# Conv-attention hybrid: the FFN's down product and fp8 cast re-placed, two mix chunks moved among the second turns

## The chip, the cores and the metric

The kernel runs on one core of one Trainium2 chip, in one launch. The metric is device time in microseconds, the median of several runs. Engines are called by name: TensorE (PE), VectorE (DVE), ScalarE (ACT), GpSimd (POOL) and SyncE (SP), which issues all DMAs of the part that is looked at here. They run side by side and are ordered only by semaphores; each executes its own list in order.

## The reference

Input x has shape (64, 55, 55, 96), float32. Cut to what matters:

```
x = conv(x) * x + bias + x               # depthwise, 9x9 taps at distance 3, centre left out
t = tokens(x)                            # (64, 3025, 96)
h = relu(bn1(ln(t) @ w1.T))              # 192 channels
X = fft(h, axis=tokens)                  # complex, 3025 points
y = real(ifft(relu(Xr*rd - Xi*id + rb) + 1j*relu(Xi*rd + Xr*id + ib)))
t = t + bn2(y @ w2.T)
u = f16(q8(ln(t)) @ q8(W1).T) + q8(b1)   # 384 channels, rounded to f16
t = t + f16(q8(relu(u)) @ q8(W2).T) + q8(b2)
```

q8 rounds to the 8-bit float with 5 exponent bits. The layer norms have no gain and no bias.

## The kernel before

Stage one is the convolution, with bands of weights as matrices. Stage two, `mixer_stage`, handles one image per part and keeps four images in flight. Part i does: the token rows of image i (`first`: transposes `turn`, product `widen`, 121-point transform `rows`), the 25-point transform `columns`, the gates and the `mix` with w2 and the `inverse` of image i-1 (`second`), the second inverse transform `inverse_rows` and the residual of image i-2 (`prep`), and the FFN of image i-3 (`third`). Parts 4 to 62 are one loop, `Fori`; parts 0 to 3 and 63 to 66 are written out with the missing pieces left away. Parts 3 to 64 have both `second` and `third`.

An image has 3025 tokens as 25 steps of 121. The FFN goes over them in seven chunks, CHUNK = 0, 4, 8, 12, 16, 19, 22, 25: four chunks of four steps and three of three. The 31 pairs of frequencies for `mix` and `inverse` are cut in seven as well: MIXED = 0, 5, 10, 15, 19, 23, 27, 31, so three chunks of five pairs and four of four. One mix pair is the products of L1034 and L1036.

On every engine a part is two halves. The first is a loop over 14 half chunks for image i, with the eight gate tiles of image i-1 put between them at TILE_AT. In it GpSimd adds and clips for the gates (L664, L667), VectorE combines them (L864, L865, L868, L875). The second half is what the change touches:

- Second turns (TensorE, L1054): seven transposes of the normalised tokens of image i-3, into banks 4 and 5; ScalarE copies each to `xq` (L748), and the turn of chunk c waits for the copy of chunk c-2. mix(0) stands ahead of turn 4. mix(0) waits for `v_ready`, `s_ready` and `d_ready` of all eight gate tiles.
- FFN loop, TensorE, slot c from 0 to 9: mix(c) unless it is 0, up(c) (L1078, three products into banks 4, 5, 6), inverse(c-1) (L1065), inverse_rows(c-3) (L958), down(c-1) (L1094, all into bank 7).
- ScalarE, slot c from 0 to 7: out_w2(c) (L757, mixed from the mix), wide(c) (L771, the up product to `y16`), out_inverse(c-1) (L763), narrow(c-1) (L779, the down product to `z16`).
- VectorE, slot c from 0 to 9: residual(c-3) (L885) and the layer-norm statistics of the chunk before it (L800), then for c below 7 the bias and relu of `y16` in place (L924, three instructions) and the cast to `hq` (L930); in slots 0 and 3 also statistics of the next image's tokens.
- GpSimd, chunk by chunk: bias b2 to `z16` (L675), sum with `t2` into `o_sb` (L678). SP stores `o_sb` to the output.

Buffers set these waits: up(c) waits for wide(c-1); wide(c) waits for the cast of chunk c-2 (`hq_ready`), since `y16` has two buffers; down(c) waits for the cast of chunk c and for narrow(c-1) (`z_ready`); the cast of chunk c waits for down(c-2) (`f2_done`); mix(c) waits for out_w2(c-2) and inverse(c) for out_w2(c); residual(c) waits for inverse_rows(c) and for `o_sb` of chunk c of image i-3 (`o_ready`), because both use `t2`. In the next part, columns(0) waits for five residuals and columns(1) for all seven.

Of the kernel before, what the change touches and what calls it, by code (L numbers as in the profile page):

```python
# [98 lines left out]
U = 121  # L99
# [7 lines left out]
NC = 7  # L107
CHUNK = (0, 4, 8, 12, 16, 19, 22, 25)
MIXED = (0, 5, 10, 15, 19, 23, 27, 31)
# [3 lines left out]
TILES = 8  # L113
KC = 8
# [4 lines left out]
LAG = 3  # L119
EARLY = 3  # L120
ROOT_C = 3
TILE_AT = (0, 2, 4, 6, 7, 9, 10, 12)


# [166 lines left out]
def mixer_stage(nc, x1, p, a_d, g_d, out):  # L291
    with ExitStack() as ctx:
# [3 lines left out]
        def sem(name):  # L296
            return ctx.enter_context(nc.semaphore(name))
# [35 lines left out]
        y16 = [sb(f"y16{s}", [128, FM, TOK], F16) for s in range(2)]  # L333
        hq = [sb(f"hq{s}", [128, FM, TOK], F8) for s in range(2)]
# [172 lines left out]

        act_passed = sem("act_passed")
        pe_passed = sem("pe_passed")
        dve_passed = sem("dve_passed")  # L510
        pool_passed = sem("pool_passed")
        sp_passed = sem("sp_passed")
        t_loaded = sem("t_loaded")
# [14 lines left out]
        s_ready = sem("s_ready")  # L528
        d_ready = sem("d_ready")
# [14 lines left out]
        relu_ready = sem("relu_ready")  # L544
        hq_ready = sem("hq_ready")
        f2_done = sem("f2_done")
# [7 lines left out]
        def ring(b, c, n=NC):  # L554

            return b * n + max(c - 1, 0)
# [96 lines left out]
        @block.gpsimd  # L653
        def _(pool):
            b2 = b2q[:, :].unsqueeze(1).broadcast_to([U, JC, C])

            def part(i, first, second, prep, third, more):
                if second:
                    b = i - 1
                    for t in range(TILES):  # L660
                        p0, p1, _, hf = group(t)
                        pool.wait_ge(m_ready, b * TILES + t + 1)
                        sv = spec[0:HH, hf, p0:p1, 0:Q // 2]
                        nc.gpsimd.tensor_tensor(sv, sv, gate_buffer(gc, t), ALU.add).then_inc(s_ready, 1)  # L664
                        pool.wait_ge(v_ready, b * TILES + t + 1)
                        pool.sem_inc(pool_passed, 1)
                        nc.gpsimd.tensor_scalar(gate_buffer(gv, t), gate_buffer(gv, t), 0.0, None,  # L667
                                                ALU.max).then_inc(v_cut, 1)
                if third:
                    b = i - 3  # L670
                    for c in range(NC):
                        pool.wait_ge(z_ready, b * NC + c + 1)
                        c0, c1 = CHUNK[c], CHUNK[c + 1]
                        z = z16[c % 2][:, 0:c1 - c0, :]
                        nc.gpsimd.tensor_tensor(z, z, b2[:, 0:c1 - c0, :], ALU.add).then_inc(z_biased, 1)  # L675
                        pool.wait_ge(z_biased, b * NC + c + 1)
                        pool.wait_ge(o_stored[c % 2], slot_uses(b, c) * 16)
                        nc.gpsimd.tensor_tensor(o_sb[c % 2][:, 0:c1 - c0, :], t2[:, c0:c1, :], z,  # L678
                                                ALU.add).then_inc(o_ready, 1)

            run_all(pool, part)
# [4 lines left out]
        def _(act):  # L686
# [6 lines left out]
            def part(i, first, second, prep, third, more):  # L693
# [46 lines left out]
                if third:  # L740
                    b = i - 3
# [32 lines left out]
                def narrow(c):  # L774
                    b = i - 3
                    act.wait_ge(f2_done, b * NC + c + 1)
                    act.wait_ge(o_ready, ring(b, c))
                    n = CHUNK[c + 1] - CHUNK[c]
                    nc.scalar.activation(z16[c % 2][:, 0:n, :].rearrange("p j c -> p (j c)"),  # L779
                                         ps[0:U, 7, 0:n * C], ACT.Copy).then_inc(z_ready, 1)  # L780

                for c in range(NC + 1):
                    if second and c < NC:
                        out_w2(c)
                    if third and c < NC:
                        wide(c)
                    if second and c:
                        out_inverse(c - 1)
                    if third and c:
                        narrow(c - 1)  # L790
                    if more and c == ROOT_C - 1:
                        root(0, i + 1)

            run_all(act, part)

        @block.vector
        def _(dve):
# [42 lines left out]
            def part(i, first, second, prep, third, more):  # L840
# [73 lines left out]
                for c in range(NC + LAG):  # L914
                    if prep and c >= LAG:
                        residual(c - LAG)
                        if c > LAG:
                            residual_stats(c - LAG - 1)
                    if third and c < NC:
                        b = i - 3  # L920
                        dve.wait_ge(y16_ready, b * NC + c + 1)
                        n = (CHUNK[c + 1] - CHUNK[c]) * U
                        for m in range(FM):
                            last = nc.vector.tensor_scalar(y16[c % 2][:, m, 0:n], y16[c % 2][:, m, 0:n],  # L924
                                                           b1q[:, m:m + 1], 0.0, ALU.add, ALU.max)
                        last.then_inc(relu_ready, 1)
                        dve.wait_ge(f2_done, ring(b, c))
                        dve.wait_ge(relu_ready, b * NC + c + 1)
                        dve.sem_inc(dve_passed, 1)
                        nc.vector.tensor_copy(hq[c % 2][:, :, 0:n], y16[c % 2][:, :, 0:n],  # L930
                                              saturate=False).then_inc(hq_ready, 1)
                    if more and c < 4 - EARLY:
                        n = EARLY + c
                        dve.wait_ge(t_loaded, (i + 2) * 16)
                        last = stats(tok, 0, PART[n], PART[n + 1])
                        if n == 3:
                            variance(0, i + 1, last)
                    if more and c == ROOT_C:
                        inverse_root(0, i + 1)
                        deviation(i + 1)  # L940
# [6 lines left out]
        def _(pe):  # L947
            def part(i, first, second, prep, third, more):
# [73 lines left out]
                            turn(h // 2 + 1)  # L1022
                def mix(c):
                    b = i - 1
                    if c == 0:
                        pe.wait_ge(v_ready, b * TILES + TILES)
                        pe.wait_ge(s_ready, b * TILES + TILES)
                        pe.wait_ge(d_ready, b * TILES + TILES)
                    if c >= 2:
                        pe.wait_ge(w2_ready, b * NC + c - 1)  # L1030
                    for p in range(MIXED[c], MIXED[c + 1]):
                        n = p - MIXED[c]
                        o = ps[0:Q, c % 2, n * C:(n + 1) * C]
                        nc.tensor.matmul(o, spec[0:HH + 1, 0, p, :], w2t[0:HH + 1, 0, :],  # L1034
                                         start=True, stop=False)
                        last = nc.tensor.matmul(o, spec[0:HH, 1, p, :], w2t[0:HH, 1, :],  # L1036
                                                start=False, stop=True)
                    last.then_inc(w2_done, 1)

                if third:  # L1040
                    b = i - 3
                    if first:
                        pe.wait_ge(turned_used, (i + 1) * NC)
                        pe.wait_ge(hid_ready, (i + 1) * HALVES)
                    else:
                        pe.wait_ge(y16_ready, b * NC)
                    for c in range(NC):
                        if second and c == 4:
                            mix(0)
                        pe.wait_ge(xn2_ready, b * NC + c + 1)  # L1050
                        if c >= 2:
                            pe.wait_ge(xq_ready, b * NC + c - 1)
                        for j in range(CHUNK[c + 1] - CHUNK[c]):
                            last = nc.tensor.transpose(ps[0:C, 4 + c % 2, 128 * j:128 * j + U],  # L1054
                                                       xn2[:, CHUNK[c] + j, :], ident[0:U, 0:U])
                        last.then_inc(turned2, 1)
# [40 lines left out]
                    last.then_inc(f2_done, 1)  # L1097

                for c in range(NC + LAG):
                    if second and c < NC and not (third and c == 0):  # L1100
                        mix(c)
                    if third and c < NC:
                        up(c)
                    if second and 1 <= c <= NC:
                        inverse(c - 1)
                    if prep and c >= LAG:
                        inverse_rows(c - LAG)
                    if third and 1 <= c <= NC:
                        down(c - 1)

            run_all(pe, part)

# [39 lines left out]
```

## Time and profile before

| | us |
|---|---|
| median of 3 runs | 6206.72 (6203.02 to 6210.03) |
| profiled execution | 6218.28 |
| its span, first to last instruction | 6216.1 |
| granted TensorE clock, mean over the span | 0.951 |
| TensorE busy with products | 5297.6 |
| VectorE busy | 4527.8 |
| ScalarE busy | 3248.1 |
| GpSimd busy | 1951.5 |

The convolution fills the time up to about 1044 us. From there on one part follows another, one image every 77.5 to 78.6 us. An engine's busy time is a sum over stages with different limits, so the rows further down are of one image, the one whose second turns begin at 3003.59 us. Times in a timeline are starts; several instructions of one group are merged into one row; pipelined products overlap, so the distance of two starts can be shorter than the duration.

### The profile page before, as it was taken

Reading aid. Unit: us, or ns where it says so; the run is one execution under the profiler, and the core shown is the slowest. Engines: PE = TensorE matmul, PEld = TensorE weight load, DVE = VectorE, ACT = ScalarE, POOL = GpSimd, SP = SyncE. Lnnn points to the kernel's source line nnn. Section 1 sums busy time; section 2 is a strip of 40 time slices with the busy share of each in tenths; the row PEclk is TensorE's granted clock in tenths of the full one; section 3 lists DMA queues with packets and bytes.
Section 4 is the critical chain, followed back from the end, with each engine's and each line's share of the span. In section 5 each row is a group of like instructions: output and inputs, shape, how many; then the busy total and the mean of one; then the engine's idle time right before and its main releaser. Section 6 shows DMA issues by size and latency. Waiting matters only on the chain. (4 is left out here: it accounts for less than half of the span.)

```text
span 6216.1 us, 136648 instructions
## 1 busy us (share of the span) xinstructions
PE 5297.6 (85%) x44298; PEld 4566.4 (73%) x44298; DVE 4527.8 (73%) x12660; ACT 3248.1 (52%) x6469; POOL 1951.5 (31%) x1924
## 2 busy tenths in 40 slices
PE   8999996488888888888888888888888888888887
PEld 8889996377777777777777777777777777777775
DVE  4555664457777777777777777777777777777776
ACT  0000000256666666666666666666666666666664
POOL 0000000123333333434333343334333333333343
PEclk9999998689999999999999999999999999999995
DMA  6665655355555555555555555555555555555552
GB/s 223 180 188 171 193 171 161 85 137 140 139 137 137 141 137 136 141 142 139 139 139 138 140 139 141 142 141 139 140 140 141 139 140 142 139 136 138 139 139 55
DMA packets 681435, 892.28 MB, mean 144 GB/s; under 512 B 240785, under 2 KB 629130, under 8 KB 659530
## 3 DMA queue, kind: packets, MB, share of 16 engines
q1 hardware_dynamic: 610124, 800.99, 50.7%
q10 hardware_dynamic: 71174, 89.35, 4.7%
q8 instruction: 100, 1.64, 0.1%
q14 instruction: 37, 0.30, 0.0%
HBM read 505.60 MB, written 384.61 MB: 143 GB/s over the span
## 5 line engine op out<-in xcount | busy, mean ns | idle before, releaser
L664 POOL TENSOR_TENSOR spec<-spec,gc 96x400 f32<-96x400 f32 (+1 forms) x512 | 488.7, 955 | 2473.3 <-DVE spec L864 2473.3
L1007 PEld LDWEIGHTS ps<-fb,acol 100*96 100x96 f32 x7936 | 778.8, 170 | 316.0 <-DVE gv L868 233.7
L1007 PE MATMUL ps<-fb,acol 100*96 100x100 f32 x7936 | 815.4, 257 | 124.2 <-DVE gv L868 116.2
L675 POOL TENSOR_TENSOR z<-z,b2q 121x384 f16<-121x384 f16 (+1 forms) x448 | 397.4, 887 | 1560.0 <-ACT z L779 1560.0
L989 PE MATMUL ps<-hid,fa 121*128 121x384 f32 (+1 forms) x1792 | 708.6, 477 | 187.5 <-DVE arow L854 106.7
L707 ACT ACTIVATE hid<-ps,rstd 121x192 f32<-121x192 f32 x1600 | 602.7, 432 | 482.8 <-PE ps L978 482.6
L1034 PE MATMUL ps<-w2t,spec 97*100 97x96 f32 x3968 | 718.2, 264 | 19.1 <-DVE spec L875 19.1
L259 DVE SCALAR_TENSOR_TENSOR xout<-cps,xin 114x351 f32<-114x351 f32 (+3 forms) x512 | 402.4, 786 | 443.0 <-PE cps L286 443.0
L1036 PE MATMUL ps<-w2t,spec 96*100 96x96 f32 x3968 | 702.3, 260 | 0.0
L667 POOL TENSOR_SCALAR gv<-gv 96x400 f32<-96x400 f32 (+1 forms) x512 | 663.9, 1297 | 106.4 <-DVE gv L868 106.3
L854 DVE COPY arow<-ps 128x384 f32<-128x384 f32 (+1 forms) x896 | 454.3, 507 | 323.9 <-PE ps L989 293.7
L282 PE MATMUL cps<-xin,toep 114*114 114x117 f32 (+3 forms) x3072 | 615.6, 283 | 85.2 <-DMA xin<-in_x 71.9
L978 PE MATMUL ps<-w1t,xnt 97*121 97x192 f32 x3200 | 680.7, 330 | 0.7 <-ACT xnt L698 0.7
L1094 PEld LDWEIGHTS ps<-w2q,hq 128*121 128x121 fp8e5 x4800 | 326.5, 139 | 420.3 <-issue 394.7
L924 DVE TENSOR_SCALAR y<-y,b1q 128x484 f16<-128x484 f16 (+1 forms) x1344 | 521.7, 444 | 120.2 <-ACT y L771 112.7
L771 ACT ACTIVATE y<-ps 128x1452 f16<-128x1452 f32 (+1 forms) x448 | 561.0, 1252 | 56.2 <-PE ps L1078 43.1
L1094 PE MATMUL ps<-w2q,hq 128*121 128x96 fp8e5 x4800 | 350.0, 222 | 269.3 <-issue 263.7
L1034 PEld LDWEIGHTS ps<-w2t,spec 97*100 97x100 f32 x3968 | 544.3, 176 | 39.6 <-issue 29.3
L286 PE MATMUL cps<-xin,toep 114*114 114x96 f32 (+1 forms) x3072 | 570.4, 268 | 0.0
L488 ACT ACT_TABLE_LOAD x1 | 1.3, 1283 | 1078.8 <-PEq L164 1078.8
L978 PEld LDWEIGHTS ps<-w1t,xnt 97*121 97x121 f32 x3200 | 514.7, 185 | 55.4 <-ACT xnt L698 1.0
L1036 PEld LDWEIGHTS ps<-w2t,spec 96*100 96x100 f32 x3968 | 537.2, 176 | 0.0
(101 smaller groups left out, 11296.9 us busy)
## 6 DMA issues: line engine op xcount, KB each, us to landing
a_d<-arow SPq DMA_DIRECT2D x256, 384.0 KB, 3.6
acol<-a_d SPq DMA_DIRECT2D x64, 1200.0 KB
grow<-g_d SPq DMA_DIRECT2D x128, 600.0 KB, 7.4
tok<-x_d SPq DMA_DIRECT2D x64, 1134.4 KB
t_res<-x_d SPq DMA_DIRECT2D x64, 1134.4 KB
acol<-a_d SPq DMA_DIRECT2D x64, 1125.0 KB
a_d<-arow SPq DMA_DIRECT2D x192, 288.0 KB, 5.1
xin<-in_x SPq DMA_DIRECT2D x256, 211.5 KB, 5.7
```

Of the source, the lines that this page charges most:

```text
L282: nc.tensor.matmul(o[0:GP, :], toep[0:GP, ch, GP:2 * GP], xs[:, pad:pad + cols], start=True, stop=False)
L286: last = nc.tensor.matmul(o[0:GP, 0:cols - step + pad], toep[0:GP, ch, 0:GP], xs[:, step + pad:], start=False, stop=True)
L667: nc.gpsimd.tensor_scalar(gate_buffer(gv, t), gate_buffer(gv, t), 0.0, None, ALU.max).then_inc(v_cut, 1)
L707: last = nc.scalar.activation(hid[h % 2][:, j, :], ps[0:U, 5 + h % 2, j * H:(j + 1) * H], ACT.Relu, scale=rstd[0][:, s0 + j:s0 + j + 1])
L771: nc.scalar.activation(y16[c % 2][:, :, 0:n], ps[:, 4:4 + FM, 0:n], ACT.Copy).then_inc(y16_ready, 1)
L924: last = nc.vector.tensor_scalar(y16[c % 2][:, m, 0:n], y16[c % 2][:, m, 0:n], b1q[:, m:m + 1], 0.0, ALU.add, ALU.max)
L978: last = nc.tensor.matmul(ps[0:U, 5 + h % 2, j * H:(j + 1) * H], xnt[c % 2][:, 2 * (h % 2) + j, :], w1t[:, :], start=True, stop=True)
L989: nc.tensor.matmul(ps[0:M, 7, 0:n * H], fa[:, :], hid[h % 2][:, 0:n, :].rearrange("p j h -> p (j h)"), start=True, stop=True).then_inc(a_d ...
L1007: last = nc.tensor.matmul(ps[0:HH, 2 - 2 * (t % 2) + n // 4, 128 * (n % 4):128 * (n % 4) + Q], acol[:, p0 + n, hf * HH:(hf + 1) * HH], fb[ ...
L1034: nc.tensor.matmul(o, spec[0:HH + 1, 0, p, :], w2t[0:HH + 1, 0, :], start=True, stop=False)
L1036: last = nc.tensor.matmul(o, spec[0:HH, 1, p, :], w2t[0:HH, 1, :], start=False, stop=True)
L1094: last = nc.tensor.matmul(ps[0:U, 7, C * j:C * (j + 1)], hq[c % 2][:, m, j * U:(j + 1) * U], w2q[:, m, :], start=(m == 0), stop=(m == FM - 1))
```

## The change

Three edits, all in the FFN half of a part.

- TensorE: the call of down moves from the end of slot c, as down(c-1), to the head of slot c, as down(c-2). ScalarE: narrow(c-1) becomes narrow(c-2), and its loop gets a ninth slot.
- mix(0) stands ahead of second turn 2 and mix(1) ahead of second turn 4. The mix of chunk c waits for the `s_ready` and `d_ready` of only those gate tiles that cover its pairs, each chunk for its own.
- The cast from `y16` to `hq` goes from VectorE to GpSimd. GpSimd's list becomes: cast 0, cast 1, then for each chunk c: cast c+2, bias c, sum c. The cast keeps its waits. The semaphore that counted VectorE's passes goes away.

```diff
@@ gpsimd
+                def cast(c):
+                    b = i - 3
+                    n = (CHUNK[c + 1] - CHUNK[c]) * U
+                    pool.wait_ge(f2_done, ring(b, c))
+                    pool.wait_ge(relu_ready, b * NC + c + 1)
+                    pool.sem_inc(pool_passed, 1)
+                    nc.gpsimd.tensor_copy(hq[c % 2][:, :, 0:n], y16[c % 2][:, :, 0:n],
+                                          saturate=False).then_inc(hq_ready, 1)
+
                 if third:
                     b = i - 3
+                    cast(0)
+                    cast(1)
                     for c in range(NC):
+                        if c + 2 < NC:
+                            cast(c + 2)
                         pool.wait_ge(z_ready, b * NC + c + 1)
@@ scalar
-                for c in range(NC + 1):
+                for c in range(NC + 2):
                     if second and c < NC:
                         out_w2(c)
                     if third and c < NC:
                         wide(c)
-                    if second and c:
+                    if second and 1 <= c <= NC:
                         out_inverse(c - 1)
-                    if third and c:
-                        narrow(c - 1)
+                    if third and c >= 2:
+                        narrow(c - 2)
@@ vector
-                        dve.wait_ge(f2_done, ring(b, c))
-                        dve.wait_ge(relu_ready, b * NC + c + 1)
-                        dve.sem_inc(dve_passed, 1)
-                        nc.vector.tensor_copy(hq[c % 2][:, :, 0:n], y16[c % 2][:, :, 0:n],
-                                              saturate=False).then_inc(hq_ready, 1)
@@ tensor
                 def mix(c):
                     b = i - 1
+                    tiles = 2 * ((MIXED[c + 1] - 1) // KC) + 2
                     if c == 0:
                         pe.wait_ge(v_ready, b * TILES + TILES)
-                        pe.wait_ge(s_ready, b * TILES + TILES)
-                        pe.wait_ge(d_ready, b * TILES + TILES)
+                    pe.wait_ge(s_ready, b * TILES + tiles)
+                    pe.wait_ge(d_ready, b * TILES + tiles)
@@ tensor, second turns
-                        if second and c == 4:
-                            mix(0)
+                        if second and c in (2, 4):
+                            mix(c // 2 - 1)
@@ tensor, FFN loop
                 for c in range(NC + LAG):
-                    if second and c < NC and not (third and c == 0):
+                    if third and 2 <= c < NC + 2:
+                        down(c - 2)
+                    if second and c < NC and not (third and c < EARLY_MIX):
                         mix(c)
                     if third and c < NC:
                         up(c)
...
                         inverse_rows(c - LAG)
-                    if third and 1 <= c <= NC:
-                        down(c - 1)
```

EARLY_MIX is 2.

## Rows read from the trace of the kernel before

**Rows 1.** The page: busy time, share of the span and instructions of each engine.
```profile
PE 5297.6 (85%) x44298; PEld 4566.4 (73%) x44298; DVE 4527.8 (73%) x12660; ACT 3248.1 (52%) x6469; POOL 1951.5 (31%) x1924
```

**Rows 2.** Waits: who waited for whom, total us, times, longest.
```profile
PE ps L1094 <- issue: 263.7, 251, 2.5
```

**Rows 3.** Timeline, TensorE, one image's FFN: start, duration, instructions, [idle before].
```profile
3003.59 0.99 PE L1054 MATMUL ps<-ident,xn 121*96 121x121 f32 x8
3005.00 1.60 PE L1054 MATMUL ps<-ident,xn 121*96 121x121 f32 x8 [0.42 <-ACT xq L748]
...
3009.26 0.78 PE L1054 MATMUL ps<-ident,xn 121*96 121x121 f32 x6
...
3011.70 0.77 PE L1078 MATMUL ps<-xq,w1q 96*128 96x484 fp8e5 x3 [0.74 <-ACT xq L748]
...
3014.07 0.78 PE L1078 MATMUL ps<-xq,w1q 96*128 96x484 fp8e5 x3
...
3015.94 0.84 PE L1094 MATMUL ps<-w2q,hq 128*121 128x96 fp8e5 x12 [0.21 <-issue]
3016.62 0.38 PE L1034 MATMUL ps<-w2t,spec 97*100 97x96 f32 x2
...
3018.42 0.78 PE L1078 MATMUL ps<-xq,w1q 96*128 96x484 fp8e5 x3
...
3023.36 0.78 PE L1078 MATMUL ps<-xq,w1q 96*128 96x484 fp8e5 x3
...
3027.64 0.63 PE L1078 MATMUL ps<-xq,w1q 96*128 96x363 fp8e5 x3
...
3031.59 0.63 PE L1078 MATMUL ps<-xq,w1q 96*128 96x363 fp8e5 x3
...
3036.15 0.63 PE L1078 MATMUL ps<-xq,w1q 96*128 96x363 fp8e5 x3
...
3042.09 0.68 PE L1094 MATMUL ps<-w2q,hq 128*121 128x96 fp8e5 x9 [2.19 <-issue]
...
3044.46 1.01 PE L969 MATMUL ps<-ident,tok 121*97 121x121 f32 x4
```

**Rows 4.** Timeline, ScalarE, the same image, same columns.
```profile
3011.08 0.47 ACT L748 ACTIVATE xq<-ps 96x363 fp8e5<-96x363 f32 x1 [0.39 <-PE ps L1054]
...
3012.50 1.38 ACT L771 ACTIVATE y<-ps 128x1452 f16<-128x1452 f32 x1 [0.50 <-PE ps L1078]
...
3020.51 0.56 ACT L763 ACTIVATE mixed<-ps 100x480 f32<-100x480 f32 x1
3022.11 0.49 ACT L779 ACTIVATE z<-ps 121x384 f16<-121x384 f32 x1 [1.04 <-PE ps L1094]
```

**Rows 5.** Groups of instructions of VectorE and GpSimd: busy us, mean ns | idle before.
```profile
L885 DVE TENSOR_TENSOR t<-ps,t_res 121x384 f32<-121x384 f32 (+1 forms) x448 | 228.5, 510 | 322.7 <-PE ps L958 287.7 <-POOL o_sb L678 34.8
...
L667 POOL TENSOR_SCALAR gv<-gv 96x400 f32<-96x400 f32 x384 | 510.4, 1329 | 82.3 <-DVE gv L868 82.3
```

**Rows 6.** Timeline, VectorE and GpSimd, the same image.
```profile
3003.73 0.57 DVE L868 SCALAR_TENSOR_TENSOR gv<-ps,nrd,gq 96x350 f32<-96x350 f32 x1
...
3013.92 0.86 DVE L924 TENSOR_SCALAR y<-y,b1q 128x484 f16<-128x484 f16 x3 [1.34 <-ACT y L771]
3020.21 0.92 DVE L930 CAST hq<-y 128x1452 fp8e5<-128x1452 f16 x1
3030.90 0.91 POOL L675 TENSOR_TENSOR z<-z,b2q 121x384 f16<-121x384 f16 x1 [1.37 <-ACT z L779]
3034.46 0.73 DVE L800 BATCH_NORM_STATS2 bn<-t 121x6 f32<-121x96 f32 x4
3039.17 0.73 POOL L675 TENSOR_TENSOR z<-z,b2q 121x288 f16<-121x288 f16 x1 [1.39 <-ACT z L779]
```

**Rows 7.** Windows: busy time (instructions) of each engine, granted clock, DMA share, GB/s.
```profile
3042.00:3047.00 5.00, 4.91 (x32) 4.28 (x33) 3.82 (x20) 0.98 (x2) 1.46 (x2) 0.66 0.38 120
3004.00:3009.00 5.00, 4.58 (x32) 4.19 (x31) 1.52 (x4) 2.17 (x4) 1.45 (x2) 0.66 0.83 186
```

More of the change, by code:

```diff
@@ L121 @@
 ROOT_C = 3
+EARLY_MIX = 2
 TILE_AT = (0, 2, 4, 6, 7, 9, 10, 12)
@@ L509, in mixer_stage @@
         pe_passed = sem("pe_passed")
-        dve_passed = sem("dve_passed")
         pool_passed = sem("pool_passed")
```

## The prediction

> **What bounds the kernel now.** I read the busy times first: TensorE leads with 85% of the span, VectorE has 73%, ScalarE 52%, GpSimd 31% [rows 1]. So the end is set by TensorE's own work and the holes in it, and GpSimd looks free. The waits come next: the largest hole of TensorE in the part that is changed stands before the down product, 263.7 us in 251 waits [rows 2], though each has a second condition that the profile only calls "issue". Third, the timeline of one image, TensorE alone [rows 3]: the FFN part of this image runs from the first up product (3011.70) to the first turn of the next part (3044.46), 32.76 us, and the rows before up(0) start at 3003.59. Idle before down products: four holes, the first of 0.21 and the last of 2.19, 4.15 us together in this image (as the total of [rows 2] over 63 images says too). Other images show the same pattern. Last the timeline of the other engines in the same stretch [rows 4, 6], for the lengths of what TensorE waits for.
>
> **The order on TensorE.** Before, slot c is: mix(c), up(c), inverse(c-1), inverse_rows(c-3), down(c-1). After, it is down(c-2), mix(c), up(c), inverse(c-1), inverse_rows(c-3). Written out in a line, both give up(c), inverse(c-1), inverse_rows(c-3), down(c-1), mix(c+1), up(c+1): down k lies between up(k+1) and up(k+2) in both. So TensorE's own order changes only by the two mixes. What does change is ScalarE: narrow(k) followed down(k) in slot k+1, and now stands in slot k+2, behind wide(k+2) and out_inverse(k+1). And down(c-1) still waits for narrow(c-2), because all down products write bank 7.
>
> **New loop 1, ScalarE.** For four tokens: up(c) takes 0.77; wide 1.38 starts 0.03 later and the next ScalarE work begins 1.28 after it starts; out_inverse 0.56 (next after 0.46), narrow 0.49, then 0.15 to the product, as between the last xq copy and up(0) (11.55 to 11.70) [rows 3, 4]. So down(c-1) starts 0.80 + 1.28 + 0.46 + 0.49 + 0.15 = 3.18 after up(c). Then 0.68 for down (15.94 to 16.62) and the mix, 1.46 for four pairs and 1.80 for five (16.62 to 18.42) [rows 3]. For three tokens the wide is 1.08 and the whole lead 2.74, 2.66 with a three-token narrow. The distances between ups become:
> up(2) to up(3): 3.18 + 0.68 + 1.46 = 5.32 against 4.94, +0.38.
> up(3) to up(4): 5.32 against 4.28, +1.04.
> up(4) to up(5): 2.74 + 0.68 + 1.46 = 4.88 against 3.95, +0.93.
> up(5) to up(6): 2.74 + 0.51 + 1.46 = 4.71 against 4.56, +0.15.
> Together +2.50 us. TensorE has only 1.5 to 2.15 us of inverse products to put under these leads. The idle that the VectorE cast caused before the middle down products is inside the old distances, so it is already credited.
>
> **The cast's price X on GpSimd.** The trace has no copy there. Nearest rows: the one-input TENSOR_SCALAR takes 1.33 us for 400 columns [rows 5], 3.3 ns a column: 4.8 us for 1452. The two-input TENSOR_TENSOR takes 0.91 us for 384 columns and 0.73 for 288 [rows 6], so 1.9 ns a column and 0.2 fixed: 2.9 us; VectorE's own cast, 0.92 us [rows 6], is the lower end. I take half of the two-input slope (one tensor read and no arithmetic): 0.93 ns x 1452 + 0.2 = 1.55 us, and 1.21 us for 1089 columns. This is the weakest number here; both ends stay in the range.
> The Trainium skill (GPSIMD Engine Reference, Engine selection) says that elementwise work belongs on VectorE, GpSimd being about twice as slow with two inputs and near line rate with one. By its line rate (1.2 GHz) the cast would be an estimated 1.2 us plus a fixed 0.2 and the sum some 30 us lower; the trace disagrees for the one-input TENSOR_SCALAR, which takes nearly three times line rate [rows 5].
>
> **down(0).** wide(0) ends 2.18 after up(0), relu 0.86 on VectorE [rows 6], 0.3 of hand-overs: down(0) starts 3.35 + X = 4.90 after up(0), up(2) 0.68 + 1.80 later, at 7.38. Before: 2.37 + 4.35 = 6.72. That is +0.66 per image. Up(1) itself is bound by wide(0), 2.3 after up(0), as before, but now nothing (before: mix(1)) lies in that hole.
>
> **The two mixes.** mix(0) and mix(1) now stand among the second turns. Mix(0) only moves within them. Mix(1) adds 1.80 there, and covers one hole of 0.42 before the third turn product and little else: the last turn still waits 0.4 for its xq copy and up(0) 0.74 for the last one [rows 3]. From the mix's end (3009.26) to up(0) it stays 2.44. I count 3003.59 to up(0) as 9.25 instead of 8.11: mixing at the low clock (this stretch has 0.66 granted [rows 7]) from 4.5 to 7.2, two turns to 8.6, mix(1) to 10.4, then 2.44: 12.84. That is +1.14. The eased waits are in this count: mix(0) no longer waits for VectorE's last join, but still for the last v_ready, whose operation ends at 3004.30 [rows 6]. If mix(0) and mix(1) run wholly at full clock the term falls to about +0.6, if the cover is worse than counted it is at most the whole mix, +1.8.
>
> **New loop 2, GpSimd and VectorE.** GpSimd runs cast(c) ahead of z(c-2) and o_sb(c-2). VectorE's residual(c-2) waits for that o_sb, and relu(c+1) stands behind it on VectorE; cast(c+1) waits for relu(c+1). So one turn of this ring is relu 0.86 (0.75 for three tokens) + X + bias and o_sb 2.0 + residual 0.5 + bn_stats 0.65 [rows 5, 6] + 0.35 of hand-overs, 4.35 + X = 5.9 us, 5.5 for three tokens. That is longer than loop 1. Counted from up(0) = 0: up(2) 7.4, up(3) 12.7, relu(3) 15.55 (held by residual(0), whose product stands behind up(3)), relu(4) 21.3, relu(5) 26.6, relu(6) 31.9, its cast ends 33.95, down(6) 34.1. Up(6) is at 27.6, so down(6) is 6.5 behind it, against 5.94 before (36.15 to 42.09): +0.55. From there to the next turn, 2.37 stays. The VectorE time freed (0.92 x 7) buys nothing, since the engine waits for GpSimd instead. No DMA is moved in its queue; only the stores of o_sb are issued later, the last one some 4 us behind the next turn, where SP has nothing but the load of t_res behind it, which residual(0) needs 40 us later. The last residual ends 4.5 behind the next turn (0.6 + 0.46 before); the second group of column products wants it 5.0 behind it (3049.51), so this just fits; were it missed by the 1 us that GpSimd's three last pairs can slip, it would cost 60 us, inside the range.
>
> **Sum.** 1.14 + 0.66 + 2.50 + 0.55 = 4.85 us for each of the 62 parts that have both mixes and an FFN (i = 3 to 64): +301 us. The profiled execution took 6218.28 us (span 6216.1) against a median of 6206.72: it would be 6519, or 6507 on the median's footing; two last parts without mixes add a few. Forecast 6510. With X = 0.92 loop 1 ends last, down(6) lies 5.05 behind up(6), and the sum is 1.14 + 0.03 + 2.50 - 0.89 = 2.8 us, 6380. TensorE's new holes (1.6 behind up(0), 1.6 before down(0) and down(1), 1.0 in later slots) may bring further stretches at the lower of its two clocks, 1.2 GHz: one fell behind the 2.19 us hole here, and 5 us at 0.66 granted [rows 7] cost 1.7. That is 0 to +1.5 us per image, up to 6600.
>
> **Rivals.**
> A, the cast costs as much as a two-input operation (X = 2.9): down(0) 1.35 later, ring 7.25 us a turn, the chance of hiding any of it gone. By the same count down(6) is at 40.45 and the sum +11.2 us: 6900. For it: every GpSimd row here is at 1.9 ns a column or more. Against it: those either read two tensors or compute.
> B, the cast costs as the TENSOR_SCALAR (X = 4.8): four casts of 4.8 and three of 3.6 are 30 us beside 12 us of bias work in a stretch of 33; GpSimd becomes the bound of the FFN part, +21 us per image, 7510. For it: the only one-input row. Against: that row clips, a copy doesn't.
> C, faster. The holes before down are the hq casts' doing, and a whole slot of lead removes them: -4.15 us, with the 0.66 filled among the turns -4.8, times 62: 5910. Its place is narrow(c-2): it decides if the ScalarE lead behind up(c) (3.18) fits under the inverse products (1.49 or 2.15). For it: the 2.19 us hole before down(6) is truly VectorE's queue. Against: bank 7 is single, and 3.18 does not fit.
> D, no change: loop 1's losses are paid by the hole before down(6) (-0.89) and a shorter low-clock stretch behind it; needs X under 0.9, and ScalarE's lead shorter by 0.5 us in each of four slots than its rows say; 6207.
>
> **Chances.** Forecast 0.50 (own range 6370 to 6610), A 0.24, B 0.15, C 0.08, D 0.03. The range takes in the forecast and A: 6370 to 6950. 0.2% (12 us) is what a measurement of this kernel can tell from no change: faster 0.08, same 0.03, slower 0.89.
>
> **What would show it.** The CAST group on GpSimd and its mean: X. The wait of the down product put to ScalarE's z copy or issue, near 1.0 us in slots 3 to 6 and 1.6 in 1 and 2. VectorE's residual waiting for GpSimd's o_sb in the middle chunks of each image (34.8 us in the whole run now [rows 5]). Distance between the fourth and fifth up products near 5.3 us, up(0) to the next turn 36.5. A period per image near 83 instead of 78 us. The forecast is wrong if down follows at once on the inverse products, or if X is above 2 us.

## The result and the profile after

The changed kernel takes 6945.09 us (median of 4 runs, 6929.87 to 6952.25) against 6208.38 for the kernel before in the same session. The ratio is 1.117 with a 95% interval of 1.113 to 1.121. It is slower, as forecast, but by 737 us and not by 301. The page after:

```profile
span 6949.3 us, 137091 instructions
...
PE 5806.5 (84%) x44298; PEld 4942.4 (71%) x44298; DVE 4051.7 (58%) x12212; ACT 3211.6 (46%) x6469; POOL 2444.9 (35%) x2372
...
PEclk9999996888888888888888888888888888888886
```

The last row of the page before, for comparison:

```profile
PEclk9999998689999999999999999999999999999995
```

Against [rows 1] TensorE does the same 44298 products and is busy 509 us longer. Its work has not grown, so the same products ran slower. The PEclk row, the granted TensorE clock in 40 slices in tenths of full speed, shows it: nearly all 9 before, 8 in every slice of the mixer now (mean over the span 0.951 before, 0.877 after). VectorE is 476 us less busy, GpSimd 493 us more, which is the cast moved.

The timeline of TensorE in one image, the rows that answer to [rows 3] (start, duration, instructions, [idle before]); L1063 is the second turns, L1087 up, L1074 inverse, L1103 down, L977 the first turn of the next part:

```profile
3064.46 0.99 PE L1063 MATMUL ps<-ident,xn 121*96 121x121 f32 x8
...
3070.87 0.49 PE L1063 MATMUL ps<-ident,xn 121*96 121x121 f32 x3 [0.43 <-ACT xq L761]
3072.10 0.77 PE L1087 MATMUL ps<-xq,w1q 96*128 96x484 fp8e5 x3 [0.74 <-ACT xq L761]
3074.43 0.77 PE L1087 MATMUL ps<-xq,w1q 96*128 96x484 fp8e5 x3 [1.56 <-ACT y L784]
3075.04 1.04 PE L1074 MATMUL ps<-mixed,ib 100*100 100x96 f32 x10
3076.84 1.45 PE L1103 MATMUL ps<-w2q,hq 128*121 128x96 fp8e5 x12 [0.76 <-issue]
...
3081.49 1.42 PE L1087 MATMUL ps<-xq,w1q 96*128 96x484 fp8e5 x3
...
3089.70 1.42 PE L1087 MATMUL ps<-xq,w1q 96*128 96x484 fp8e5 x3
...
3096.04 0.63 PE L1087 MATMUL ps<-xq,w1q 96*128 96x363 fp8e5 x3
...
3100.82 0.63 PE L1087 MATMUL ps<-xq,w1q 96*128 96x363 fp8e5 x3
...
3105.43 0.63 PE L1087 MATMUL ps<-xq,w1q 96*128 96x363 fp8e5 x3
...
3112.58 0.68 PE L1103 MATMUL ps<-w2q,hq 128*121 128x96 fp8e5 x9 [1.88 <-issue]
...
3114.72 1.01 PE L977 MATMUL ps<-ident,tok 121*97 121x121 f32 x4
```

Read the durations first: the same up product of four tokens takes 0.77 at 3072 and 3074 and 1.42 at 3081 and 3089. Between 3076 and 3093 TensorE runs at half clock. It begins behind four holes in six microseconds, 0.43, 0.74, 1.56 and 0.76. From up(0) to the next turn it is 42.62 us, against 32.76 before and 36.5 predicted. The same two stretches in windows (busy of PE, PEld, DVE, ACT, POOL, then granted clock, DMA share, GB/s), first the slow stretch, then the whole image:

```profile
3076.00:3093.00 17.00, 15.11 (x88) 13.53 (x88) 3.35 (x14) 6.16 (x10) 5.32 (x5) 0.50 0.41 114
3064.46:3153.00 88.54, 74.41 (x549) 61.49 (x548) 53.76 (x175) 50.05 (x101) 38.20 (x38) 0.88 0.49 122
```

0.50 is the lower level, 1.2 GHz, for 17 us of each image of 88.5 us. In [rows 7] such stretches were short, 3 to 4 us each.

The image of [rows 3] and [rows 7] is not a usual one, and this matters further down. It has two stretches at the lower clock and takes 78.55 us, close to the longest. Of the 59 whole images of that profile, 23 have two such stretches (78.5 us on average), 16 have one (77.6) and 20 have none (75.9). So the images take 75.7 to 78.6 us, not 77.5 to 78.6, and 77.36 on average. The table has means over 59 images, worked out from the starts of the products in each profile; the last column is the time at the lower clock in one image.

| kernel | second turns to up(0) | up(0) to next turn | next turn to next second turns | image | low |
|---|---|---|---|---|---|
| before | 7.44 | 32.42 | 37.50 | 77.36 | 3.6 |
| before, the 20 images without a low stretch | 7.03 | 32.00 | 36.83 | 75.87 | 0 |
| changed | 7.82 | 42.99 | 38.31 | 89.12 | 22.1 |

The new waits can be read too. Groups of GpSimd that answer to [rows 5], and who waits for whom:

```profile
L675 POOL CAST hq<-y 128x1452 fp8e5<-128x1452 f16 x256 | 357.1, 1395 | 1471.2 <-DVE y L937 1387.1 <-issue 84.1
...
L675 POOL CAST hq<-y 128x1089 fp8e5<-128x1089 f16 x192 | 209.7, 1092 | 421.4 <-DVE y L937 392.9 <-issue 28.5
```
```profile
DVE t L898 <- POOL o_sb L691: 682.6, 304, 3.8
...
ACT z L792 <- POOL o_sb L691: 248.6, 65, 4.3
...
PE ps L1103 <- ACT z L792: 205.3, 289, 1.9
```

The cast costs 1.40 us. VectorE's residual waits for GpSimd's sum 682.6 us instead of 34.8 [rows 5], ScalarE's z copy waits for the same sum, and the down product now waits for that z copy; before, the view of waits has no such row.

### The profile page after: what moved, and what is told of

It is laid out like the page before. It is cut to its first block and busy times, and to the rows that moved or that the text cites. A ratio compares the mean times of both kernels' runs of the same rounds, so it can differ in the third digit from the quotient of the medians.

```text
span 6949.3 us, 137091 instructions
## 1 busy us (share of the span) xinstructions
PE 5806.5 (84%) x44298; PEld 4942.4 (71%) x44298; DVE 4051.7 (58%) x12212; ACT 3211.6 (46%) x6469; POOL 2444.9 (35%) x2372
## 5 line engine op out<-in xcount | busy, mean ns | idle before, releaser
L675 POOL CAST hq<-y 128x1452 fp8e5<-128x1452 f16 (+1 forms) x448 | 566.8, 1265 | 1892.6 <-DVE y L937 1780.0
L898 DVE TENSOR_TENSOR t<-ps,t_res 121x384 f32<-121x384 f32 (+1 forms) x448 | 230.7, 515 | 1238.6 <-POOL o_sb L691 682.6
L997 PE MATMUL ps<-hid,fa 121*128 121x384 f32 (+1 forms) x1792 | 710.4, 478 | 216.7 <-DVE arow L867 135.6
L1043 PE MATMUL ps<-w2t,spec 97*100 97x96 f32 x3968 | 819.0, 295 | 3.3 <-DVE gv L881 3.3
L1103 PEld LDWEIGHTS ps<-w2q,hq 128*121 128x121 fp8e5 x4800 | 395.5, 171 | 585.5 <-issue 585.5
L1045 PE MATMUL ps<-w2t,spec 96*100 96x96 f32 x3968 | 799.3, 290 | 0.0
L1103 PE MATMUL ps<-w2q,hq 128*121 128x96 fp8e5 x4800 | 443.6, 253 | 366.1 <-ACT z L792 205.3
L770 ACT ACTIVATE mixed<-ps 100x384 f32<-100x384 f32 (+1 forms) x448 | 233.8, 522 | 1039.8 <-PE ps L1045 1039.8
L937 DVE TENSOR_SCALAR y<-y,b1q 128x484 f16<-128x484 f16 (+1 forms) x1344 | 363.7, 328 | 498.8 <-ACT y L784 491.3
L1043 PEld LDWEIGHTS ps<-w2t,spec 97*100 97x100 f32 x3968 | 635.9, 206 | 6.0 <-DVE gv L881 4.3
L1045 PEld LDWEIGHTS ps<-w2t,spec 96*100 96x100 f32 x3968 | 632.8, 205 | 0.0
L1074 PEld LDWEIGHTS ps<-mixed,ib 100*100 100x100 f32 x3968 | 534.9, 210 | 67.2 <-ACT mixed L770 31.0
```

The costliest lines, as they stand in the source:

```text
L675: nc.gpsimd.tensor_copy(hq[c % 2][:, :, 0:n], y16[c % 2][:, :, 0:n], saturate=False).then_inc(hq_ready, 1)
L997: nc.tensor.matmul(ps[0:M, 7, 0:n * H], fa[:, :], hid[h % 2][:, 0:n, :].rearrange("p j h -> p (j h)"), start=True, stop=True).then_inc(a_d ...
L1074: last = nc.tensor.matmul(ps[0:Q, 2, n * C:(n + 1) * C], ib[:, p, :], mixed[:, p, :], start=True, stop=True)
L1103: last = nc.tensor.matmul(ps[0:U, 7, C * j:C * (j + 1)], hq[c % 2][:, m, j * U:(j + 1) * U], w2q[:, m, :], start=(m == 0), stop=(m == FM - 1))
```

## The experiments

Each kernel ran beside the kernel before on the same chip. The kernel before took 6211.65 us in the session of e1 to e4, 6227.34 in that of e9, e5, e6 and e8, and 6220.99 in that of e10, e11, f2 and f3; differences and ratios below are to these, unless the text names another kernel. Two theories stood against each other. K: the waits cost what was predicted, and the rest is TensorE's clock, which falls behind the hole that mix(1) left behind up(0). W: the waits alone cost it all, and the clock is a symptom.

**e1_mixes: the mix edit alone.**
```diff
-                        if second and c == 4:
-                            mix(0)
+                        if second and c in (2, 4):
+                            mix(c // 2 - 1)
...
-                    if second and c < NC and not (third and c == 0):
+                    if second and c < NC and not (third and c < EARLY_MIX):
```
(with the eased waits of `mix`)

> The kernel before with the mix edit alone: mix(0) and mix(1) among the second turns, eased waits; cast on VectorE, down and narrow as before. Theory K (clock): taking mix(1) away from between up(0) and up(1) leaves a hole of about 1.6 us behind up(0) in every image, and TensorE's clock falls to its lower level behind it for a stretch of some 17 us as in the changed kernel; this costs 6 to 7 us per image: about 6600 us. Theory W (waits): the loss of the changed kernel is all in its new waits on ScalarE and GpSimd, the mixes cost nothing or gain 0.5 us per image: 6180 to 6280 us, clock 0.95.

Measured: 6702.35 us against 6211.65, ratio 1.080 (1.076 to 1.084), clock 0.868. The hole and the fall in its trace, timeline of TensorE:

```profile
3088.99 0.49 PE L1056 MATMUL ps<-ident,xn 121*96 121x121 f32 x3 [0.43 <-ACT xq L749]
3090.22 0.77 PE L1080 MATMUL ps<-xq,w1q 96*128 96x484 fp8e5 x3 [0.74 <-ACT xq L749]
...
3092.56 0.77 PE L1080 MATMUL ps<-xq,w1q 96*128 96x484 fp8e5 x3 [1.56 <-ACT y L772]
...
3094.46 1.26 PE L1096 MATMUL ps<-w2q,hq 128*121 128x96 fp8e5 x12 [0.25 <-issue]
...
3098.93 1.42 PE L1080 MATMUL ps<-xq,w1q 96*128 96x484 fp8e5 x3
```

and the 18 us from 3094 in windows, same columns as above:

```profile
3094.00:3112.00 18.00, 17.75 (x109) 15.63 (x108) 8.89 (x27) 7.76 (x12) 3.64 (x5) 0.53 0.37 113
```

The image shown here is one of 20 of 59 in which the clock falls behind the hole of 0.25 us. In the other 39 it falls 1.1 to 1.6 us behind up(0), in the hole of 1.56 us itself, and up(1) is slow already:

```profile
3007.07 1.37 PE L1080 MATMUL ps<-xq,w1q 96*128 96x484 fp8e5 x3 [1.56 <-ACT y L772]
```

Every one of the 59 images has the long low stretch. No cast, no down and no narrow is changed here, TensorE is busy for 17.75 of the 18 us, and 491 us, two thirds of the loss, are there. W falls; whether it is the hole or something else about the moved mixes, e9 decides.

**e2_narrow: the down and narrow edit alone.**
```diff
-                    if third and c:
-                        narrow(c - 1)
+                    if third and c >= 2:
+                        narrow(c - 2)
```
(with ScalarE's ninth slot, and down(c-2) at the head of TensorE's slot)

> The kernel before with the down and narrow edit alone (TensorE's order comes out unchanged, narrow stands one slot later on ScalarE). K and the prediction's loop 1: holes of about 1.0 us before the down products of slots 3 to 6, +2.5 us less 0.9 us at the last down product, +1.6 to +2.5 us per image: 6310 to 6360 us, clock near 0.95 since mix(1) still fills the hole behind up(0). W: more than that, 6400 us and above, at an unchanged clock. Rival C of the prediction (more lead removes the holes): below 6100 us.

Measured: 6302.99 us, ratio 1.015 (1.013 to 1.018), clock 0.953; +91 us, 1.5 per image. In the trace all 44298 products of TensorE come in the same order as in the kernel before. The waits of TensorE:

```profile
PE ps L1094 <- ACT z L779: 264.6, 305, 1.9
...
PE ps L1094 <- DVE hq L930: 72.2, 67, 2.5
```

Before, the down product waited 269 us in all, nearly all of it [rows 2]; here it is 351 us (264.6, 72.2, and 14.1 put down to issue), and mostly the z copy ends it. The 82 us more are most of the 91. Loop 1 is real and small, as predicted.

**e3_cast: the cast on GpSimd alone**, ahead of bias and sum as in the changed kernel.
```diff
+                        if c + 2 < NC:
+                            cast(c + 2)
                         pool.wait_ge(z_ready, b * NC + c + 1)
```
(and VectorE's cast gone)

> The kernel before with the cast on GpSimd alone, in the changed kernel's order on GpSimd (cast c+2 ahead of bias c). Loop 2 with X = 1.4 us: one turn of the ring relu, cast, bias, sum, residual, statistics is 5.75 us against up distances of 4.3 to 4.9 before, so about +3 us per image, 6400 us; the clock stays near 0.95. W expects 6500 us or more. If GpSimd's cast only relieves VectorE: 6100 us or less.

Measured: 6442.97 us, ratio 1.037 (1.033 to 1.040), clock 0.936; +231 us, 3.7 per image, against an expected +3. The waits show the ring of loop 2 (VectorE's residual waits for GpSimd's sum, which stands behind a cast):

```profile
DVE t L897 <- POOL o_sb L690: 885.5, 324, 3.8
ACT z L791 <- POOL o_sb L690: 777.3, 316, 4.3
```

An image spends 6.9 us at the lower clock here, instead of 3.6. Yet the three images without a low stretch are no shorter than the rest (80.60 us against 80.75 on average), so it is the ring that sets the time, not this clock. Against the images before that have no low stretch either (75.87 us), the ring costs 2.3 us between up(0) and the next turn (34.25 against 32.00) and 2.5 us more in the first half of the next part (39.31 against 36.83).

**e4_fill: the changed kernel, one hole filled.**
```diff
                     last.then_inc(f1_done, 1)
+                    if c == 0 and second:
+                        for m in range(4):
+                            nc.tensor.matmul(ps[0:Q, 3, 0:2 * Q], ib[:, m, :],
+                                             ib[:, 0:2, :].rearrange("p a b -> p (a b)"),
+                                             start=True, stop=True)
```

> The changed kernel with four dummy products of constants (100x100 by 200 columns, float32, into bank 3, which nothing reads then) behind up(0), in the hole where TensorE waits for wide(0); nothing of the computation is changed. K: the clock does not fall behind up(0) or falls later and shorter, mean clock up from 0.88 to about 0.95, time down by up to 6 us per image: 6500 to 6650 us. W: no gain, 6945 us or a little more.

Measured: 6691.12 us, ratio 1.078 (1.074 to 1.081) to before, clock 0.928. Work was added and 254 us went. This is less than the 295 to 445 expected: in 48 of 59 images the clock now falls later in the part, 11 to 12 us behind up(0), for 6.8 us.

**e9_mixfill: the mix edit alone, its hole filled** with the same four products.

> The kernel with the mix edit alone plus four dummy products of constants (into bank 3, nothing of the computation changed) behind up(0). If the hole behind up(0) is what lowers the clock for 17 to 20 us in each image: mean clock back to about 0.95 and 6180 to 6300 us, against 6702 without the dummies. If something else of the mix edit costs the time (the mixes' place, their operands, the eased waits): 6700 us or more.

Measured: 6222.92 us, ratio 0.999 (0.997 to 1.002), clock 0.960. All of the 491 us of e1 are gone, and no image has a long low stretch. The products in the hole, timeline of TensorE:

```profile
3005.54 0.77 PE L1080 MATMUL ps<-xq,w1q 96*128 96x484 fp8e5 x3 [0.74 <-ACT xq L749]
3006.15 1.52 PE L1085 MATMUL ps<-ib 100*100 100x200 f32 x8
3007.88 0.77 PE L1080 MATMUL ps<-xq,w1q 96*128 96x484 fp8e5 x3 [0.21 <-ACT y L772]
...
3012.27 0.78 PE L1080 MATMUL ps<-xq,w1q 96*128 96x484 fp8e5 x3
```

up(1) starts 2.34 behind up(0), as in e1, so the wait itself is untouched; only the idle is gone, and up(2) takes 0.78 and not 1.42. Within the noise of some 15 us the mixes' new place costs nothing by itself. Two small effects are in that sum. At full clock the second turns to up(0) take 7.64 us instead of 7.03, so the new place costs 0.6 us in an image; but the low stretch that lay on the mixes in 23 of 59 images before [rows 3] is gone in all but one.

**e5_mixback: the changed kernel without the mix edit.** mix(0) goes back ahead of turn 4, mix(1) into slot 1.

> The changed kernel with mix(0) ahead of turn 4 and mix(1) in slot 1 as before; down, narrow and the cast stay changed. Theory K: without the hole behind up(0) the clock holds; loops 1 and 2 are left, the edits alone gave +91 and +231 us: 6450 us if loop 1 lies inside loop 2, 6530 us if they add. Theory W (waits alone): within 100 us of 6945.

Measured: 6541.67 us, ratio 1.051 (1.045 to 1.057), clock 0.940. The loops add: 91 + 231 = 322, and 6541.67 less the 6227.34 of its session is 314. All three edits together don't quite: 91 + 231 + 491 = 813 against 737.

**e6_poollast: the changed kernel, GpSimd's order altered.**
```diff
-                        if c + 2 < NC:
-                            cast(c + 2)
                         pool.wait_ge(z_ready, b * NC + c + 1)
...
                                                 ALU.add).then_inc(o_ready, 1)
+                        if c + 2 < NC:
+                            cast(c + 2)
```

> The changed kernel with GpSimd's order alone altered: cast c+2 behind bias and sum of chunk c. Loop 2 goes, loop 1 and the hole behind up(0) stay: the hole before down(6) shrinks by 1.5 to 2 us per image, about 6830 us, clock still 0.88. If it falls to 6600 us or below, loop 2 and not the hole behind up(0) carried the loss.

Measured: 6712.93 us, ratio 1.078 (1.072 to 1.084), clock 0.887. Down by 232 us, twice the expected 115, and the size of e3's loss. Loop 2 was worth more than I gave it, and the fall behind up(0) stays, in all 59 images. The first half of the next part takes 36.83 us again, as in the images before without a low stretch.

**e8_castlast: the kernel before with the cast on GpSimd in this other order.**

> The kernel before with the cast on GpSimd, but on GpSimd cast c+2 stands behind bias and sum of chunk c. Loop 2 theory: residual c no longer waits behind a cast, so the +231 us of the cast edit go, and VectorE is 6 us per image freer, which shortens the hole before down(6): 6130 to 6230 us. If it is the cast's own length or its hold on the memory port shared with VectorE: 6400 us or more, as with the other order.

Measured: 6073.25 us, ratio 0.975 (0.970 to 0.980), clock 0.959: faster than before, and by more than expected. The rival of its expectation, that the cast's own length or its contention with VectorE is the cost, falls. The same cast, on the same engine and of the same length, costs 231 us in one place of GpSimd's list and gains 154 in the other. Its groups on GpSimd, and TensorE's waits for the down product and the next largest:

```profile
L674 POOL CAST hq<-y 128x1452 fp8e5<-128x1452 f16 x256 | 356.7, 1394 | 807.1 <-DVE y L936 735.7 <-issue 67.9 <-PE ps L1101 3.5
```
```profile
PE ps L1101 <- issue: 201.3, 191, 1.6
PE ps L1014 <- DVE gv L880: 116.8, 192, 2.2
```

263.7 us of waiting before down [rows 2] became 201.3, and an image spends 2.2 us at the lower clock, against 3.6 before.

**e10_fillmore: the changed kernel, three holes filled** (four dummy products behind up(0), two ahead of down(0), four ahead of down(1)).
```diff
                 def down(c):
                     b = i - 3
+                    if c <= 1 and second:
+                        for m in range(2 + 2 * c):
+                            nc.tensor.matmul(ps[0:Q, 3, 0:2 * Q], ib[:, m, :],
...
```
(with the four products of e4)

> The changed kernel with dummy products of constants (bank 3, nothing of the computation changed) in three holes of each image: four behind up(0), two ahead of the wait of down(0), four ahead of that of down(1). With one hole filled it took 6691 us at clock 0.93. If the rest above the waits' own cost is the clock: clock 0.94 to 0.96 and 6480 to 6560 us, which is also where the prediction's sum without a further clock fall lay (6480 with the cast at its measured 1.40 us). If more holes filled give nothing, 6690 us.

Measured: 6522.16 us, ratio 1.049 (1.046 to 1.051), clock 0.957. One image on TensorE:

```profile
4014.98 0.77 PE L1087 MATMUL ps<-xq,w1q 96*128 96x484 fp8e5 x3 [0.74 <-ACT xq L761]
4017.31 0.77 PE L1087 MATMUL ps<-xq,w1q 96*128 96x484 fp8e5 x3 [0.21 <-ACT y L784]
...
4022.21 0.78 PE L1087 MATMUL ps<-xq,w1q 96*128 96x484 fp8e5 x3
...
4027.52 0.78 PE L1087 MATMUL ps<-xq,w1q 96*128 96x484 fp8e5 x3
...
4032.83 0.63 PE L1087 MATMUL ps<-xq,w1q 96*128 96x363 fp8e5 x3
...
4037.61 0.63 PE L1087 MATMUL ps<-xq,w1q 96*128 96x363 fp8e5 x3
...
4042.23 0.63 PE L1087 MATMUL ps<-xq,w1q 96*128 96x363 fp8e5 x3
...
4051.37 1.01 PE L977 MATMUL ps<-ident,tok 121*97 121x121 f32 x4
```

At full clock this is the schedule of the prediction: 5.31 and 5.31 between ups where 5.32 stood, 4.78 and 4.62 for 4.88 and 4.71, and 36.39 from up(0) to the next turn for 36.5. The means of this run, in the columns of the table above:

| kernel | second turns to up(0) | up(0) to next turn | next turn to next second turns | image | low |
|---|---|---|---|---|---|
| three holes filled | 7.72 | 36.08 | 38.30 | 82.10 | 3.3 |

The third column is 0.80 longer than before, and 1.5 longer than in the images before without a low stretch; the two images of this run without one take even 39.1. In it the product of the next image's 121-point transform (L997, before L989) waits longer for VectorE's copy `arow`. The rows are of the kernel before, of this run, and of e6 for comparison, whose order on GpSimd is the other one:

```profile
PE ps L989 <- DVE arow L854: 106.7, 192, 1.3
PE ps L997 <- DVE arow L867: 136.9, 256, 1.5
PE ps L997 <- DVE arow L867: 108.7, 193, 2.5
```

**e11_mixfill2: the mix edit alone, its hole half filled**, two dummy products instead of four.

> The mix edit alone with two dummy products behind up(0) instead of four: the hole of 1.56 us is filled to about half. If any part of idle time there counts, the clock falls in some images: between 6223 (four dummies) and 6702 us (none). If there is a sharp limit, it lands on one of the two.

Measured: 6237.07 us, ratio 1.003 (1.001 to 1.005), clock 0.959. Half of the filling is almost as good as all of it: the loss does not shrink in step with the idle. The long low stretch appears in 2 of 59 images, against all 59 in e1 and none in e9.

**f2_fill6: the kernel before, its hole of 2.19 us ahead of the last down product filled** with four dummy products into bank 1.

> The kernel before with four dummy products (bank 1, nothing of the computation changed) ahead of the last down product, in the hole of 2.19 us. The stretch of 3 to 4 us at the lower clock behind that hole goes: 1.5 us per image, about 6110 us, clock 0.97. If the fall comes from elsewhere: 6210 us.

Measured: 6148.47 us, ratio 0.990 (0.987 to 0.992), clock 0.963: 73 us gained by four products that compute nothing, less than the 111 expected.

**f3_castlast_mix0: the candidate**, e8 with mix(0) ahead of turn 2, mix(1) left in slot 1.

> Candidate: the cast on GpSimd behind bias and sum (6073 us so far) plus mix(0) ahead of second turn 2 with the eased waits, mix(1) left in slot 1 so that no hole opens behind up(0). Mix(0) covers the hole of 0.42 us ahead of turn 2 and no longer waits for the last join: 0.3 to 0.7 us per image, 6030 to 6060 us. If the clock falls all the same, 6100 us and above.

Measured: 6059.18 us, ratio 0.974 (0.971 to 0.976), clock 0.963. This is the fastest of all and beats both kernels; its lead over e8 (14 us, intervals that overlap) is not shown.

## Why the prediction was wrong

**Right: TensorE's order and loop 1.** Apart from the two mixes the order did not change (e2), and the up distances of loop 1 came out within 0.1 us wherever the clock was full (e10, and 4.78 and 4.61 in the changed kernel's own last slots).

**Right: loop 2, and X.** 1.40 us against my 1.55. The two forms give (1395 - 1092) ns / 363 columns = 0.83 ns a column and 0.18 us fixed. The Trainium skill (GPSIMD Engine Reference, Engine selection) calls one-input work roughly line rate, and by that the trace agrees for the cast. For the TENSOR_SCALAR of [rows 5] it still doesn't (3.3 ns a column, four times as much and not "nearly three times"), so that row was no measure for a copy, and rivals A and B, which lived on such rows, fell. The time landed where A put it (6900) for another reason: a number that fits doesn't show its mechanism. In down(6) the count gave 6.5 behind up(6), the trace has 7.15 after, 6.56 in e10.

**Half right: the price of loop 2.** Alone and inside the change it is 231 us, 3.7 per image, where the prediction's own terms for it (0.66 + 0.55 per image, and the 0.9 that it keeps loop 1 from gaining back) come to 2.1 x 62 = 130. Between up(0) and the next turn, at full clock, it measures 2.3 (e3), so these terms hold. What they lack lies behind the next turn, where the prediction let the last residual "just fit" and added nothing. The column products, which it watched, do fit (VectorE's residual ends 1.7 us of their waits in the whole changed run). But the rows product waits for VectorE's `arow` copies, as the rows in e10 show, and it stops doing so when GpSimd's order is altered (e6). That VectorE comes late to them because it is held by the ring until the end of the part is the likely chain; no run isolates it.

**Wrong: the clock's term, "0 to +1.5 us per image".** The sum stood at 6510 with this as an addition, and it was about 7 us per image: the changed kernel took 6945 us and the same kernel with its three holes filled 6522, 423 us less, or 436 when each is compared with the kernel before of its own session, over 62 parts. The step priced the fall by the one stretch that [rows 7] showed, 5 us at 0.66. Behind up(0) the stretch lasts 17 to 20 us, and it begins ahead of work, where 15 of 17 us were products and each took nearly twice as long. I had listed the hole of 1.6 us behind up(0) with the others and asked only whether the clock falls again, not how long it stays low or what it lies on.

**Wrong with it: the mixes' term, +1.14.** I worked it out from an image in which a low stretch lay on the mixes and took it for the usual one; 36 of 59 images have none there. The count of 9.25 came out as 7.64 (3064.46 to 3072.10): mix(0) took 1.8 us and not 2.7, the turns between the mixes 0.8 and not 1.4, both at full clock. Like against like, the edit costs 0.6 us in its own place at full clock (7.64 against 7.03), and 0.2 to 0.4 on average, since it removes that low stretch (7.64 in e1 and 7.82 in the changed kernel against 7.44). But by taking mix(1) out of the hole behind up(0) it cost 7.7 us per image in the next one (e1 less e9, 479 us). The prediction saw the empty hole, noted that up(1) comes at the same time with or without it, and left it among the holes of the clock's term.

**Rival C** fell as predicted: bank 7 is single, and down waits for the z copy (e2).

Of the 737 us, then, 436 go when the three holes are filled, and 301 stay (e10 against its own before). That these 301 equal the prediction's sum to the microsecond is luck. Per image, against the means before, e10 is 0.28 longer from the second turns to up(0), where 1.14 stood; 3.66 longer from up(0) to the next turn, where 0.66 + 2.50 + 0.55 = 3.71 stood; and 0.80 longer in the first half of the next part, where nothing stood. The middle one is a hit, the outer two are misses that cancel. The whole is also measured against a kernel that loses 1.5 us in an image to its own low stretches (77.36 against 75.87), and the dummy products of e10 may hide some of that.

What stays open is why the clock recovers after 3 to 4 us in some stretches, after 6.8 in others (e4) and after 17 to 20 behind up(0); no run varied that.

## What to carry to other kernels

Work that fills a hole whose end is set by another engine looks free to move away, since the next instruction starts no earlier and no later. On TensorE it was not free here: the idle that it left lowered the clock for the work behind it. So look for holes that stand close together, and price a fall by what lies behind it at half speed. When a step goes to another engine, its place in that engine's list can matter more than its duration: here 385 us lay between two places of the same cast (231 lost, 154 gained). Put it behind whatever somebody else's queue waits for. And before one image is taken as the measure, compare it with the others.

## What the runs showed of the hardware

- Holes of 0.43, 0.74 and 1.56 us close together (and in a third of the images a fourth of 0.25) lowered the clock from 2.4 to 1.2 GHz in all 59 images (e1); with the 1.56 partly filled by two products it fell so in 2 of 59 (e11), with four in none (e9).
- A stretch at 1.2 GHz lasted 3 to 4 us in most places, 6.8 us in some (e3, e4), and 17 to 20 us behind up(0), with TensorE busy 17.75 of 18 us (e1).
- Dummy products made a kernel faster: 73 us on the kernel before (f2), 423 to 436 us on the changed one (e10).
- GpSimd's copy from f16 to fp8 is 0.83 ns a column and 0.18 us fixed, its TENSOR_SCALAR on f32 took 1.33 us for 400 columns, 3.3 ns each [rows 5].
